# A perceiver block on one core: order of the Mamba input products, the second norm moved into the scan's stage, and an earlier load of the MLP's first weights

## What is computed

```python
def _ssm(h, ...):                                   # h = rmsnorm(layernorm(x), norm1_w)
    xin, z = split(einsum('bld,ed->ble', h, in_proj_w), 2)      # 1024 channels each
    xin = silu(causal_conv4(xin) + conv_b)                      # depthwise, 4 taps
    dt, Bm, Cm = split(einsum('bld,ed->ble', xin, x_proj_w), [32, 48])
    delta = softplus(einsum('blr,dr->bld', dt, dt_proj_w) + dt_proj_b)
    A = -exp(A_log)
    # over t:  h = exp(delta*A)*h + (delta*x)*B ;  y = sum_n h*C      (16 states)
    y = ys + xin * D
    return einsum('bld,ed->ble', y * silu(z), out_proj_w)
x = x + _ssm(...)
h = rmsnorm(x, norm2_w)
x = x + (silu(h @ w1.T) * (h @ w3.T)) @ w2.T
```

## Time and profile before

| | us |
|---|---|
| median of 3 runs | 2579.02 (2578.78 to 2579.15) |
| the profiled execution, its own time | 2580.78 |
| its span, first to last instruction | 2579.0 |
| mamba_inputs, first to last instruction | 1832.9 to 1901.6 |
| mamba_scan | 1902.5 to 2126.9 |
| second_norm | 2127.7 to about 2141.3 (the end of its DMA traffic) |
| gated_mlp starts | 2142.6 |

### The profile page before, as it was taken

One profiled execution on the slowest core, in us unless ns is written; L12 is line 12 of the kernel. 1 busy time (PEld: TensorE's weight loads), 2 busy tenths in 40 slices (PEclk: granted clock), 3 DMA queues, 4 the chain that ended last, 5 costly groups with the idle time before them and its releaser, 6 DMA issues. The chain is left out here.

```text
span 2579.0 us, 39421 instructions
## 1 busy us (share of the span) xinstructions
PE 2407.2 (93%) x14143; PEld 1016.4 (39%) x14143; DVE 1981.5 (77%) x1986; ACT 1595.5 (62%) x1964; POOL 681.0 (26%) x471
## 2 busy tenths in 40 slices
PE   7999999999999799999999999999857778988988
PEld 3333333333333244444444444444322233444444
DVE  5777777777777788888988888887669983358876
ACT  5555555555564478787878788786354432238884
POOL 1455555565554400000000000000049970020001
PEclk9999999999999899999999999999878898999999
DMA  6245644554453773333334333331240005168993
GB/s 244 82 148 168 204 148 146 186 179 156 146 157 104 188 225 96 100 98 98 98 90 110 102 96 100 99 97 50 107 164 1 0 1 196 49 240 334 376 362 130
DMA packets 177959, 366.02 MB, mean 142 GB/s; under 512 B 19490, under 2 KB 90275, under 8 KB 174179
## 3 DMA queue, kind: packets, MB, share of 16 engines
q1 hardware_dynamic: 176290, 360.75, 44.1%
q0 software_dynamic: 1280, 4.20, 0.5%
q10 hardware_dynamic: 322, 0.21, 0.0%
HBM read 254.24 MB, written 106.68 MB: 140 GB/s over the span
## 5 line engine op out<-in xcount | busy, mean ns | idle before, releaser
L452 DVE TENSOR_REDUCE kv_mx<-kv_s 128x1024 f32 (+1 forms) x512 | 595.3, 1217 | 224.6 <-PE kv_s L488 224.6
L795 DVE TENSOR_TENSOR at_pl<-at_pf,at_ph 128x1024 f16<-128x1024 f32 x512 | 613.1, 1223 | 116.1 <-ACT at_ph L742 107.2
L748 ACT ACTIVATE at_pf<-at_st 128x1024 f32<-128x1024 f32 x512 | 497.5, 1025 | 189.6 <-PE at_st L913 153.5
L912 PE MATMUL at_st<-keep_big,at_k_cur 128*128 (+1 forms) x1024 | 391.1, 382 | 11.9 <-DMA at_k_one<-kd 9.4
L913 PE MATMUL at_st<-keep_big,at_k_one 128*128 (+1 forms) x1024 | 389.4, 380 | 0.0
L742 ACT ACTIVATE at_ph<-at_pf 128x1024 f16<-128x1024 f32 x256 | 272.8, 1066 | 0.0
L1101 POOL MEMSET mi_xp<- 128x24 f32 x1 | 0.1, 123 | 945.8 <-POOLq L60 945.8
L876 PE MATMUL at_acc<-at_ph,at_vs 128*128 128x512 f16 x1024 | 242.6, 379 | 2.9 <-DVE at_pl L795 2.8
L368 POOL TENSOR_TENSOR kv_ksl<-kv_kf,kv_ksh 128x512 f16<-128x512 f32 x128 | 147.7, 1154 | 247.3 <-ACT kv_ksh L396 247.3
L1021 PE MATMUL kv_kp<-first_ch,first_wkh 128*128 128x512 f16 x512 | 195.4, 382 | 4.5 <-DVEq L434 4.5
L1021 PE MATMUL kv_kp<-first_ch,first_wkl 128*128 128x512 f16 x512 | 195.3, 381 | 0.0
(11 more groups left out here) (346 smaller groups left out, 3884.1 us busy)
## 6 DMA issues: line engine op xcount, KB each, us to landing
keep_big<-gate_up SPq DMA_DIRECT2D x17, 2048.0 KB, 10.5
at_k_cur<-kd SPq DMA_DIRECT2D x128, 256.0 KB, 3.8
at_vs<-vd SPq DMA_DIRECT2D x64, 512.0 KB, 3.9
vd<-kv_vs SPq DMA_DIRECT2D x15, 2048.0 KB, 7.7
kv_tf<-wpack SPq DMA_DIRECT2D x21, 1024.0 KB, 6.3
keep_big<-down SPq DMA_DIRECT2D x17, 1024.0 KB
first_cf<-ctxT SPq DMA_DIRECT2D x16, 1024.0 KB, 12.7
at_k_one<-kd SPq DMA_DIRECT2D x64, 256.0 KB, 4.4
```

The lines of the kernel that those rows point to most:

```text
L452: nc.vector.reduce_max(mx[:, bass.ds(g * (NH * TT) + 2 * (m - TT), 2)], s1[:, m % 3, :, :], AX.X).then_inc(s1_max, 1)
L748: nc.scalar.activation(pf[:, s % FULL, :, :], st[:, s % HP % NST, :, :], ACT.Exp, scale=SCORE).then_inc(pf_ready, 1)
L795: nc.vector.tensor_tensor(pl[:, s % RING, :, :], pf[:, s % FULL, :, :], ph[:, s % RING, :, :], ALU.subtract).then_inc(pl_ready, 1)
L912: nc.tensor.matmul(st[:, w % NST, e, :], k_cur[:, tile], qh[:, q], start=True, stop=False)
```

## The change

In `mamba_inputs` PE makes x, the first z product, all of `x_proj`, the second z product, then the delta products between the parts of the third, and then the five last z products. The delta products have four banks (`xdp`'s among them) in place of two. The first tap moves from DVE to ACT. The Silu table is loaded at the stage's start by a two-element instruction. The six last z chunks are taken raw, three by DVE and three by ACT at the stage's end; Silu over all six, in place, is one instruction of 3072 columns on ACT in the scan, behind pass 3. The convolution no longer waits for the two loads of small weights.

In the scan's stage POOL's first `b` waits until DVE's is made. The last `low` is on DVE. The second norm is part of this stage: statistics of a tile follow its addition, normed rows go into the `hc` buffers, transposed rows into the free halves of `hs` and into `yp`. The stage `second_norm` is gone. SP loads `w1`'s half behind the last `b` (B is free) and `w3`'s behind the last product with C.

```diff
@@ mamba_inputs, scalar
-            after = {c + 1 + c // 2: c for c in range(DIC)}
-            for f in range(LAST):
-                take(f)
-                if f in after:
-                    conv_out(after[f])
+            act.wait_ge(pad, 1)
+            nc.scalar.activation(warm[:, :], keep.zero[:, :], ACT.Silu)
...
+            for f in range(DIC):
+                act.wait_ge(p_ready, f + 1)
+                nc.scalar.activation(xp[:, f, 3:], zp[:, f % 4, :], ACT.Copy, scale=UNSCALE).then_inc(p_read, 1)
+                act.wait_ge(p_read, f + 1)
+                nc.scalar.activation(soft[:, f, :], xp[:, f, 0:T], ACT.Copy, scale=cw[:, f, 0:1]).then_inc(tap_ready, 1)
+                if f:
+                    conv_out(f - 1)
+            conv_out(DIC - 1)
+            gate(DIC, ACT.Silu)
...
+            for f in ACT_Z:
+                gate(f, ACT.Copy)
@@ mamba_inputs, vector
-                own.done(nc.vector.tensor_scalar(c, xp[:, f, 0:T], cw[:, f, 0:1], None, ALU.mult))
...
+            for f in DVE_Z:
+                dve.wait_ge(p_ready, f + 1)
+                nc.vector.tensor_scalar(keep.zs[:, f - DIC, :], zp[:, f % 4, :], UNSCALE, None,
+                                        ALU.mult).then_inc(z_read, 1)
@@ mamba_inputs, tensor
+            for f in range(DIC + 1):
+                project(f)
+            pe.wait_ge(small_in, 32)
+            for c in range(DIC):
+                x_proj(c)
+            project(DIC + 1)
...
+            delta(range(0, 4))
+            project(DIC + 2, slice(0, 6))
+            delta(range(4, 6))
+            project(DIC + 2, slice(6, 12))
+            delta(range(6, 8))
+            for f in range(DIC + 3, 2 * DIC):
+                project(f)
@@ mamba_scan, sync
+            sp.dma_start(nw[:, :], n2w).then_inc(n_in, 16)
+
+            sp.wait_ge(b_ready, NP - 1)
+            load_gates(sp, keep, wsplit, slice(0, DF // 2), next_in, (0,))
+            sp.wait_ge(dve_hc, NP - pool_passes(NP))
+            sp.wait_ge(pool_hc, pool_passes(NP))
+            load_gates(sp, keep, wsplit, slice(0, DF // 2), next_in, (1,))
+            sp.wait_ge(next_in, 64)
@@ mamba_scan, gpsimd
+                if i == 1:
+                    pool.wait_ge(first_ready, 1)
...
-            low(DIC - 1)
@@ mamba_scan, scalar
+                if i == 3:
+                    nc.scalar.activation(keep.zs[:, NOW_Z:, :], keep.zs[:, NOW_Z:, :], ACT.Silu).then_inc(zs_ready, 1)
@@ mamba_scan, vector
             for t in range(TT):
                 dve.wait_ge(o_ready, t + 1)
-                nc.vector.scalar_tensor_tensor(keep.a[:, t, :], tiles[t], UNSCALE, keep.a[:, t, :],
-                                               ALU.mult, ALU.add)
+                own.done(nc.vector.scalar_tensor_tensor(keep.a[:, t, :], tiles[t], UNSCALE, keep.a[:, t, :],
+                                                        ALU.mult, ALU.add))
+                own.done(nc.vector.bn_stats(st[:, t, :], keep.a[:, t, :]))
+                own.inc(nc.vector.bn_aggr(mv[:, t, :], st[:, t, :]))
```

More of the change, by code:

```diff
@@ L1037 @@
 PASSES = DS // HN
+NOW_Z = 2
 POOL_OUT = (1, 4)
@@ L1112, in conv_out, with gate @@
                 nc.scalar.activation(xih[:, c, :], keep.xin[:, c, :], ACT.Copy, scale=SA).then_inc(xih_ready, 1)
[L1115 removed]
+            def gate(f, func):
                 act.wait_ge(p_ready, f + 1)
[L1117 to L1121, removed]
[L1123 to L1127 removed]
+                nc.scalar.activation(keep.zs[:, f - DIC, :], zp[:, f % 4, :], func, scale=UNSCALE).then_inc(p_read, 1)
+            act.wait_ge(pad, 1)
+            nc.scalar.activation(warm[:, :], keep.zero[:, :], ACT.Silu)
+            act.wait_ge(conv_in, 48)
+            act.wait_ge(pad, 2)
+            for f in range(DIC):
[7 more added lines that the diff above has]
+            gate(DIC, ACT.Silu)
             act.wait_ge(xd_ready, 1)
[L1129 removed]
+            nc.scalar.activation(xd[:, :], xdp, ACT.Copy, scale=UNSCALE).then_inc(xd_read, 1)
             act.wait_ge(xd_read, 1)
@@ L1132, in _ @@
                 nc.scalar.activation(ds[n * DR:(n + 1) * DR, :], xd[0:DR, :], ACT.Copy, scale=SA).then_inc(dh_ready, 1)
-            take(LAST)
+            gate(DIC + 1, ACT.Silu)
             act.wait_ge(xin_ready, DIC)
@@ L1191, in x_proj @@
                 pe.wait_ge(xil_ready, c + 1)
-                last = product(nc, xdp[:, :], three(xpw[0][:, c, :], xpw[1][:, c, :], xih[:, c, :], xil[:, c, :]),
+                last = product(nc, xdp, three(xpw[0][:, c, :], xpw[1][:, c, :], xih[:, c, :], xil[:, c, :]),
                                start=(c == 0), stop=(c == DIC - 1))
@@ L1329, in _ @@
                     high(f - 1)
+                if i == 3:
+                    nc.scalar.activation(keep.zs[:, NOW_Z:, :], keep.zs[:, NOW_Z:, :], ACT.Silu).then_inc(zs_ready, 1)
             high(DIC - 1)
+            act.wait_ge(var_ready, 1)
+            nc.scalar.activation(rows.sd[:, :], rows.var[:, :], ACT.Sqrt).then_inc(sd_ready, 1)
+            act.wait_ge(nws_ready, 1)
+            for c in range(DC):
+                act.wait_ge(hT_ready, c + 1)
+                nc.scalar.activation(keep.hh[:, c, :], hT[c], ACT.Copy, scale=nws[:, c:c + 1]).then_inc(hh_ready, 1)
         @block.vector
@@ L1469 @@
+            pe.wait_ge(y_ready, DIC)
+            pe.wait_ge(h_ready, TT)
+            for c in range(DC):
+                for t in range(TT):
+                    last = nc.tensor.transpose(hT[c][:, t * P:(t + 1) * P], h_rows[t][:, c * P:(c + 1) * P], ident[:, :])
+                last.then_inc(hT_ready, 1)
 NE = 16
```

165 lines of the change are left out of this document (77 added, 88 removed).

## The result

| | before | after |
|---|---|---|
| median of six runs each (lowest to highest) | 2578.85 (2574.78 to 2579.15) | 2558.94 (2554.82 to 2563.47) |
| the profiled execution, its own time | 2580.78 | 2556.76 |
| its span | 2579.0 | 2555.0 |

The ratio is 0.9926, 95% interval 0.9913 to 0.994: the change makes the kernel 19.9 us faster, and the predicted 2560.2 is 1.3 us above the median. The profiled execution is one of the quicker ones; its span is 24.0 us shorter than that of before, not 19.9. (A span is 1.8 us less than the same execution's time, in both kernels.)

A forecast was written before the change was run, and what follows sets the result against it. It took the serial chain through mamba_inputs to the scan, and DVE in the scan, as bounds. Gains of 15.7 + 0.3 + 2.35 + 0.4 = 18.8 us took 2579.0 to 2560.2, range 2556.5 to 2564.5.

The forecast's parts named there:

- Inputs, 15.7 predicted: mamba_inputs: first delta product 16.3 us earlier, less 0.6 for ACT's three last copies ending behind DVE; gain 15.7.
- Scan, 0.3: Scan stage: net gain 0.3 us, from an earlier start less a loss by ACT's Silu before pass 4.
- The start: Scan's start: DVE's first b alone takes 1.23 us, not 3.42, so the first multiplication by C gains 1.6.
- the Silu's wait: Scan, pass 4: DVE waits for ACT, delayed by the new Silu and two table loads; loss 1.3 us.
- Norm and MLP's start, 2.35: Second norm to MLP: early gate weights, no barrier and scaling off the chain start the MLP 2.35 us sooner.
- The MLP's first product, 0.4: MLP's first product on PE: shorter idle time improves its clock, gaining 0.4 us (bounds 0 and 1.9).
- drain at table loads: ACT's table switches in the scan cost 2.66 us each, including a 1.38 drain; time 2563.0; chance 0.05.
- DVE's saving not reached: mamba_inputs: ACT, PE's order or z banks set the pace, or PE's clock falls in x_proj; near 2571; chance 0.06.
- The scan at the lower clock: Scan: PE at clock 0.50 becomes the bound, adding up to 62 us, 2622; chance 0.02.
- nothing gained: Softplus lands under late z products, x_proj is slow and the Silu stalls more passes; 2576 to 2582; chance 0.02.

The follow-up runs named there:

- delta_late: Changed kernel with four more z products on PE ahead of the eight delta products, in place of behind and between them; median 2572.05 us.
- pool_free: Changed kernel without POOL's wait for DVE's first b, so POOL's second b runs beside it; profiled twice, medians 2561.49 and 2558.07 us.
- no_silu: Changed kernel without the Silu of six z chunks on ACT at pass 3 and its two table loads; median 2557.56 us.
- b_early_load: Kernel before, with only the MLP's gate weights issued early, in the scan's stage; second norm keeps its stage and barrier; median 2575.94 us.
- before_again: Kernel before, unaltered, run for a second profile; median 2578.88 us.
- after_again: Changed kernel, unaltered, run for a second profile; median 2559.99 us.
- tap_dve: Changed kernel with the convolution's first tap back on DVE and none on ACT; median 2564.49 us.
- best_warm2: best_warm with 32 in place of 30 idle matmuls ahead of the norm's transposes and nine more behind them; median 2557.97 us.
- best_warm: Changed kernel with a sixth z chunk on DVE, interleaved norm statistics and 30 unread PE matmuls before the norm's transposes; median 2555.13 us.

## Why the prediction was right

Measured against the earlier trace rows, with the sum's own steps, at the MLP's first gate:

- *Inputs, 15.7 predicted*: 15.86. The first delta product came 16.35 earlier (16.3), the three copies, which end 0.44 behind DVE (0.6), took that back. ACT's tap takes 0.72 (0.71 was taken), and delta_late shows that the chain, not PE's total, was the bound.
- *Scan, 0.3*: 0.16 at the last gate. The start gave 1.81 (1.6) and the Silu's wait was 1.34 (1.3); DVE's waits for PE, 5.21 before and 5.47 after, took another 0.26. The mechanism of the start is shown by both pool_free profiles, that of the Silu by no_silu. At pass 8 the gain is 0.38, in both profiles to 0.01. That the last gate is as near is luck in part: profiles with this scan have it at 213.40 to 214.77.
- *Norm and MLP's start, 2.35*: 2.29. By b_early_load 2.08 of it is the early issue (1.85 against before_again).
- *The MLP's first product, 0.4*: 1.93. **This step failed.** I took the two outcomes, 4.68 and 2.75, for the ends of a range and chose a value near one end. But no profile lies between 2.75 and 4.02. Seven profiles have the same tail to 0.02 us (after, after_again, tap_dve, delta_late, pool_free twice, no_silu): in three the clock was back before the product (2.75), in four it came back inside it (4.03 to 4.38). The mean of the seven is 3.59, so against the 4.75 of before (two profiles) the change is worth 1.2 there on the average, not 0.4, and 1.93 in this profile. That the profile of after has the better outcome is luck.

The four measured terms make 20.24, against 18.8; with 1.2 for the product they make 19.5, near the 19.9 of the medians. To the 20.24 the profile adds 0.22 from a stage that started earlier and 3.54 behind the MLP's first gate, together the 24.0 of the span; the last part is the experts' spread and no effect of the change. With before's 431.6 behind the gate, after would have had a span of 2558.5 and so a time of 2560.3, to be compared with the 2580.78 of before's profile; they are 1.4 and 1.9 above their kernels' medians. That my start of 2579.0, a span, was also the median is a coincidence: before's profiled execution was 1.8 us slower than the runs that I had.

The rivals: *drain at table loads* is refuted. The Silu starts 1.30 after the start of its table load, and the exponential 1.29 after that of the next. The Trainium skill ("ScalarE: Activation LUTs", What ACT_TABLE_LOAD costs) gives 2.66 for a switch; here the instruction behind it starts after 1.3, and the wait at pass 4 fits 1.28 a load. no_silu agrees: 1.2 to 1.3 us earlier, not 4. *DVE's saving not reached* did not come (chunks 2.84 apart), but tap_dve shows that its clock mechanism is real and 0.5 us a chunk away, though it slowed one product and not seven. *The scan at the lower clock* did not come (0.88 as before), and neither did *nothing gained*.

## What to carry to other kernels

When an engine is full, ask which part of its work the next stage needs: here 11 us came without an instruction saved on PE, for the most part by moving z products behind the delta products, and another 5 by taking one of four instructions of the convolution off DVE, which paced it. Weights for the next stage can be loaded as soon as the buffers' last reader has gone, which is often long before the stage ends; by itself that was about 2 of the tail's 2.3 us. When a product may meet either level of the clock, write both outcomes with their chances in place of a value between, and judge edits of 1 or 2 us by landmarks in the profile, since a stage far behind them spreads the total by 9 us.

## What the runs showed of the hardware

- The granted clock doesn't answer to PE's idle time at once, nor at the same distance each time. In after PE ended the output projection at 2109.95 and the clock fell in 2112 to 2116 (0.91 there, 0.50 next); in the seven profiles with the same tail the fall came 2.1 to 5.3 us behind PE's last product. In tap_dve the first product at 2126.83 still had 0.50, in after the one at 2124.11 had 1.00, though the tails are 16.05 and 16.06 us long. What decides between the two no run shows.
- Matmuls whose results nobody reads held it, in one profile each: 1.00 from the output projection to the MLP with 41 of them (best_warm2), while 30 moved the fall behind the transposes (best_warm).
- DVE's b and POOL's, issued in the same moment with both inputs in SBUF, took 3.42 and 5.62 for one and two instructions; DVE's alone takes 1.22.
